# A fused perceiver layer: the Gelu of a small network moved from the scalar engine's table to a polynomial and a tanh, and unread matrix products put into two places

## The reference

```
qk = einsum('bhqd,bhkd->bhqk', Q, K);  scores = qk / sqrt(dk)
feats  = stack([mean(scores), mean(max(scores)), mean(var(softmax(scores)))])   # 3 numbers a head
hidden = gelu(feats @ w1.T + b1, approximate=False)       # 64 wide, erf form
hidden = gelu(hidden @ w2.T + b2, approximate=False)      # 64 wide
t = exp(clip(hidden @ w3.T + b3, log 0.1, log 10))        # one number a head
out = (softmax(qk / (2 t)) @ V) @ Wo.T + bo
```

## Time and profile before

| what | us |
|---|---|
| median of 3 runs | 1217.95 |
| lowest, highest | 1214.53, 1223.5 |
| profiled execution, first to last instruction (span) | 1213.1 |
| VectorE busy | 812.4 (67%) |
| ScalarE busy | 765.5 (63%) |
| TensorE's mean granted clock | 0.897 |

### The profile page before, as it was taken

The page is one execution under the profiler, slowest core; times in us unless marked ns, Lnnn a source line. Parts: engine busy times, 40 slices in busy tenths (PEclk is TensorE's granted clock), DMA queues, the critical chain, the costliest instruction groups (busy, mean ns, idle before and its releaser), DMA issues.

```text
span 1213.1 us, 39205 instructions
## 1 busy us (share of the span) xinstructions
PE 1101.5 (91%) x14964; PEld 892.8 (74%) x14964; DVE 812.4 (67%) x2128; ACT 765.5 (63%) x1547; POOL 406.0 (33%) x420
## 2 busy tenths in 40 slices
PE   3867799999999999999999999999999999999864
PEld 3535587878888787878878797878787887867743
DVE  4467667566776776677777776577667777578245
ACT  2434576776766676767766776667767676766521
POOL 2268352223232331433232332333143233331223
PEclk9968798987979897989999898989889898989787
DMA  4610010201010111102010111102020100000000
GB/s 132 193 29 27 23 37 4 61 11 42 19 44 21 36 29 28 37 2 54 11 45 20 37 29 29 36 4 61 2 54 11 45 20 19 3 2 6 8 2 9
DMA packets 46812, 38.85 MB, mean 32 GB/s; under 512 B 14576, under 2 KB 46000, under 8 KB 46640
## 3 DMA queue, kind: packets, MB, share of 16 engines
q1 hardware_dynamic: 46640, 36.41, 11.1%
HBM read 34.30 MB, written 2.10 MB: 30 GB/s over the span
## 4 chain that ended last, share of the span: by engine, by line
PE 75%; DVE 12%; issue 5%; ACT 4%; DMA 2%; POOL 1%; SPq 1%; DVEq 0%; ACTq 0%; POOLq 0%
PE pjp L665 14%; PE s1p L704 14%; PE s2p L735 13%; PE pjp L658 12%; PE pvp L752 8%; DVE est L1392 3%; DVE negm L1386 2%; PE tlp L848 2%; PE tlp L866 1%; PE tlp L787 1%; ACT ering L1045 1%; PE tlp L842 1%; PE s2p L725 1%; PE s2p L645 1%; PE tlp L809 1%
## 5 line engine op out<-in xcount | busy, mean ns | idle before, releaser
L1386 DVE TENSOR_REDUCE negm<-s1p 128x1 f32<-128x400 f32 (+1 forms) x512 | 289.8, 566 | 199.1 <-PE s1p L704 196.6
L1045 ACT ACTIVATE ering<-s1p,negm 128x400 f32<-128x400 f32 (+1 forms) x512 | 303.8, 597 | 118.6 <-DVE negm L1386 112.2
L1056 ACT ACTIVATE pring<-s2p 128x512 f32<-128x512 f32 x427 | 240.8, 565 | 148.1 <-PE s2p L735 145.1
L704 PE MATMUL s1p<-kt,qbd 32*128 32x400 f32 (+1 forms) x1024 | 305.2, 608 | 28.1 <-ACT ering L1045 26.1
L1392 DVE BATCH_NORM_STATS2 est<-ering 128x6 f32<-128x400 f32 (+1 forms) x512 | 290.7, 568 | 19.6 <-ACT ering L1045 19.6
L735 PE MATMUL s2p<-q2bd,kt 32*128 32x128 f32 (+1 forms) x3192 | 244.6, 285 | 0.0
L735 PEld LDWEIGHTS s2p<-q2bd,kt 32*128 32x128 f32 (+1 forms) x3192 | 233.3, 194 | 5.8
L658 PE MATMUL pjp<-cr,wkv 128*128 128x256 f32 (+1 forms) x1344 | 192.4, 295 | 29.7 <-DVE vt L1358 19.2
L1264 POOL TENSOR_TENSOR cr<-stage,cr 128x512 fp32r<-128x512 f32 (+1 forms) x112 | 132.1, 1180 | 234.3 <-ACT cr L1036 234.3
L658 PEld LDWEIGHTS pjp<-cr,wkv 128*128 128x128 f32 x1344 | 171.8, 198 | 45.5 <-issue 29.1
L665 PE MATMUL pjp<-wkv,cr 128*128 128x256 f32 (+1 forms) x1200 | 195.7, 318 | 10.0 <-ACT kt L1018 9.8
(11 more groups left out here) (278 smaller groups left out, 1033.1 us busy)
## 6 DMA issues: line engine op xcount, KB each, us to landing
stage<-in_ctx SPq DMA_DIRECT2D x96, 256.0 KB, 3.0
qbd<-q_dram SPq DMA_DIRECT2D x128, 8.0 KB, 1.8
stage<-in_ctx SPq DMA_DIRECT2D x16, 65.0 KB, 2.5
vt<-in_x SPq DMA_DIRECT2D x1, 1024.0 KB, 6.8
q_dram<-late SPq DMA_DIRECT2D x1, 1024.0 KB, 4.6
late<-in_x SPq DMA_DIRECT2D x7, 128.0 KB, 2.3
out_y<-late SPq DMA_DIRECT2D x7, 128.0 KB, 1.8
late<-in_gate SPq DMA_DIRECT2D x1, 768.0 KB, 4.9
```

Source lines behind the costliest of these rows:

```text
L704: nc.tensor.matmul(s1p[u % 3][:, 0:w], qbd[s.par][rows, g, :], kt[s.par][rows, g, lo:lo + w], start=True, stop=True).then_inc(s1_full, 1)
L1045: nc.scalar.activation(ering[:, u % 3, 0:w], s1p[u % 3][:, 0:w], ACT.Exp, bias=negm[s.par][:, p, c:c + 1]).then_inc(s1_exp, 1)
L1056: nc.scalar.activation(ring_place(s, v)[0:m, 0:n], s2_bank(s, v)[0:m, 0:n], ACT.Exp).then_inc(s2_exp, 1)
L1386: nc.vector.tensor_reduce(negm[s.par][:, p, ch:ch + 1], s1p[u % 3][:, 0:w], AX.X, ALU.max, negate=True).then_inc(s1_max, 1)
```

## The change

Gelu is no longer a function of the scalar engine. With v = product + bias, VectorE makes x = v/2, q = 2x² and, by a polynomial of degree 6 in q, y = x·r(q); ScalarE takes tanh(y), and VectorE ends with (tanh + 1)·x. These are 9 operations on VectorE (`GE_N`), 1 on ScalarE and 1 more on VectorE for each of the two layers, on 128x16 tiles. q, the last step of the polynomial and the tanh lie in columns 16 to 47 of bank `tlp`. `w1m`, `w2s`, `w3b` and `hid` are 128 wide in place of 64, with zeros that GpSimd writes in the set-up.

The second layer moves from step 6 to 7, the third from 7 to 9, parts 2 and 3 of the statistics from 8 and 10 to 9 and 11, the exponential between them from 9 to 10. The rounding's operations at position 68 move to 69, step 5 of an odd slot. `keep_clock` issues products of `wkv` with itself into an `s2p` bank that the next `scores2` overwrites: 12 in odd slots and 5 in even ones ahead of the second layer, and 4 at step 13 behind the shift's.

```diff
-STATS_AT = [1, 3, 8, 10]
-MLP_AT = {5: 0, 6: 1, 7: 2}
+STATS_AT = [1, 3, 9, 11]
+MLP_AT = {5: 0, 7: 1, 9: 2}
+FILL_FOR = 8
+FILL_1 = {1: 12, 2: 5}
+FILL_MORE = 4
-W_AT, GELU_AT, C_AT = 2, 5, 9
+W_AT, C_AT = 2, 10
+GELU_AT = [5, 7]
+HALF_R = [2.0 * 2.0 ** k * c for k, c in enumerate(ERF_R)]
+GE_N = len(HALF_R) + 2
+Q_LAST = 69
...
-        w1m = sb("w1m", [P, 3, DH])
+        w1m = sb("w1m", [P, 3, P])
...
+            def keep_clock(s, n, at):
+                s_, v = s.second(at, 0)
+                if s_.has(1, B) and not s_.drains():
+                    need(pe, s2_exp, s_.lin(S2U, v - 1 - S2U))
+                    for _ in range(n):
+                        nc.tensor.matmul(s2_bank(s_, v)[:, 0:D], wkv[:, 0, 0, 0, 0:P], wkv[:, 1, 0, 0, :], start=True,
+                                         stop=True)
...
-                        if step in MLP_AT and s.has(1, B):
-                            temperature(s, MLP_AT[step])
...
-                    if step % 2 == 1 and step in MLP_AT and s.has(1, B):
+                    if step in MLP_AT and s.has(1, B):
+                        if MLP_AT[step] == 1:
+                            keep_clock(s, FILL_1[s.r], FILL_FOR)
                         temperature(s, MLP_AT[step])
+                    if step + 1 == S2_AT[0]:
+                        keep_clock(s, FILL_MORE, step + 1)
...
-            def gelu(s, n):
-                need(act, mlp_full, s.lin(N_MLP, n + 1 - N_MLP))
-                nc.scalar.activation(hid[:, n, :], tlp[0:DH, 0:H], ACT.Gelu,
-                                     bias=col("b1" if n == 0 else "b2", 0, DH)).then_inc(mlp_free, 1)
+            def gelu_tanh(s, n):
+                need(act, ge, s.lin(2 * GE_N, GE_N * (n + 1) - 2 * GE_N))
+                nc.scalar.activation(tlp[:, H:2 * H], gy[:, :], ACT.Tanh).then_inc(ge_th, 1)
...
+            def gelu(s, n, part):
+                x, b = gx[:, n, :], col("b1" if n == 0 else "b2")
+                q, low = tlp[:, H:2 * H], tlp[:, 2 * H:3 * H]
+                if part == 0:
+                    need(dve, mlp_full, s.lin(N_MLP, n + 1 - N_MLP))
+                    c = Chain(ge, s.lin(2 * GE_N, GE_N * n - 2 * GE_N))
+                    c(nc.vector.tensor_scalar(x, tlp[:, 0:H], b, 0.5, ALU.add, ALU.mult))
+                    c(nc.vector.scalar_tensor_tensor(out=q, in0=tlp[:, 0:H], scalar=b, in1=x, op0=ALU.add, op1=ALU.mult))
+                    c(nc.vector.tensor_scalar(gu[:, :], q, HALF_R[-1], HALF_R[-2], ALU.mult, ALU.add))
+                    c(nc.vector.tensor_tensor(gu[:, :], gu[:, :], q, ALU.mult))
+                    for r in HALF_R[-3:0:-1]:
+                        c(nc.vector.scalar_tensor_tensor(out=low if r == HALF_R[1] else gu[:, :], in0=gu[:, :], scalar=r,
+                                                         in1=q, op0=ALU.add, op1=ALU.mult))
+                    c(nc.vector.scalar_tensor_tensor(out=gy[:, :], in0=low, scalar=HALF_R[0], in1=x, op0=ALU.add,
+                                                     op1=ALU.mult), False)
+                    assert c.n == GE_N
+                else:
+                    need(dve, ge_th, s.lin(2, n + 1 - 2))
+                    nc.vector.scalar_tensor_tensor(out=hid[:, n, :], in0=q, scalar=1.0, in1=x, op0=ALU.add,
+                                                   op1=ALU.mult).then_inc(mlp_free, 1)
```

50 lines of the change are left out of this document (32 added, 18 removed).

## The result

The changed kernel takes 1279.74 us, the median of 4 runs (1278.48 to 1283.41), beside 1216.51 us for the kernel before on the same chip (4 runs, 1214.53 to 1223.5). The ratio is 1.0503, with a 95% interval from 1.0464 to 1.0542: 5% slower, where I had forecast 1.6% faster. The profiled execution has a span of 1276.6 us against 1213.1, 63.5 us more.

A forecast was written before the change was run, and what follows sets the result against it. TensorE was taken as the bound (75% of the chain), slowed by low clock around the Gelu waits. 1213.1 - 17.5 (even slots) - 4 (odd) + 2 (batch 16) = 1193.6 us span, plus 4.85: 1198.4 us, range 1192 to 1206.

The forecast's parts named there:

- The replay: Step-by-step timing of batches 8 and 9 after the change; in batch 8 it put unit 11 1.5 us ahead.
- surcharge for PSUM: VectorE's PSUM reads: the skill's 0.065 us an operation, estimated 16 us in all, was left out of the count.
- From there the old kernel spent 1.8 us up to 608.3: Even slots behind unit 11: full clock saves 0.9 and 1.7 us, less 0.55 us for four products; 2.5 us taken.
- the sum: Whole span: seven even slots x 2.5, eight odd x 0.5, batch 16 2 us later; 1193.6 us span, 1198.4 us median.
- Statistics and shift are not late in this: Even slot: part 3 of the statistics ends near 610, some 0.5 us ahead of the shift's turn on TensorE.
- Stand in a wait that is longer, below, and are free: TensorE: the 12 or 5 products ahead of the second layer (1.66 or 0.69 us) cost nothing.
- one more odd slot: Batch 15 was counted among the eight odd slots, each 0.5 us shorter.
- 4.85 us between span and median: Difference added to the forecast span of 1193.6 us to give the forecast median of 1198.4 us.
- The clock still falls behind the second layer: Rival: TensorE's gaps there still lower the clock and products only cost; 10.4 us slower, 1228 us; chance 0.09.
- VectorE as the bound: Rival: 2.25 us a chain and 0.1 us more a hand-over lose 14 us of the gain; 1213 us; chance 0.12.
- Theory A: Follow-up theory, not forecast: the change only moves the half-clock stretch to steps 10 to 13, where it costs much.
- Theory C: Follow-up theory, not forecast: VectorE's chain costs by its own length.

The follow-up runs named there:

- kernel 1: Changed kernel without any of the unread clock-holding products: 1264.84 us, ratio 1.0408.
- 5: Changed kernel without the four unread products at step 13: 1265.59 us, ratio 1.0348.
- 11: 6 (Gelu polynomial of four coefficients, clip's exponential behind) without any unread product: 1202.05 us, ratio 0.987.
- 14: 6 without the four products at step 13, keeping those ahead of the second layer: 1214.44 us, ratio 0.9934.
- kernel 13: kernel 2 (full chain of nine, clip's exponential behind) without any unread product: 1228.67 us, ratio 1.0039.
- 8: kernel 2 without the four products at step 13: 1243.36 us, ratio 1.019.
- kernel 9: Kernel before the change, with only the clip's exponential placed behind the second pass's on ScalarE: 1217.66 us, ratio 0.999.
- Kernel 18: kernel 12 with the clip's exponential back ahead of the second pass's (1254.02 us), plus the third layer ahead of step 9's projection on TensorE: 1234.07 us, ratio 1.0115.
- kernel 2: Changed kernel with the clip's exponential moved behind the second pass's and the first pass's on ScalarE: 1251.15 us, ratio 1.0264.
- 6: kernel 2 with four of seven polynomial coefficients, three VectorE operations fewer per chain, rougher Gelu: 1228.78 us, ratio 1.0049.
- kernel 12: 11 with four coefficients fitted anew, Gelu error below 3e-5, same instructions: 1205.22 us, ratio 0.9826.
- kernel 4: Kernel before the change, old Gelu, with only the unread products added (12 or 5, and 4 at step 13): 1236.59 us, ratio 1.0143.
- kernel 16: kernel 12 with two polynomial coefficients, chains of four operations in place of six: 1215.03 us, ratio 0.9954.
- kernel 3: Changed kernel with nine more unread products in step 10: 1275.18 us, ratio 1.0503.
- kernel 7: kernel 2 with the four unread products moved from step 13 into step 10, ahead of the second pass: 1266.39 us, ratio 1.0368.

## Why the prediction was wrong

**What held.** The chain of nine takes 1.95 us, from 608.87 to 610.82 in batch 8 (1.9 counted); the table loads are gone but for the first; the projection at step 9 takes 1.63 and 1.68 us (1.7 forecast); unit 10 comes 7.5 us behind the first layer in batch 8 (7.7 counted) and unit 11 8.3 us (8.4 counted). The replay was right as far as it went. Unit 11 of the kernel before is at 607.29, where the replay put 606.95, so at that unit the change was 1.9 us ahead, not 1.5. In the changed kernel all ten of a layer's operations read PSUM, where the prediction counted eight. No surcharge for PSUM came out: operations with a column take 0.23 and 0.24 us, the others 0.17, as those with SBUF inputs do. (The Trainium skill, "VectorE: DVE Perf Modes", TRN2 errata, would have them 0.065 us longer from PSUM, the estimate in the prediction; at 16 columns the rows don't show it.)

```profile
608.87 0.23 DVE L1501 TENSOR_SCALAR gx<-tlp,cols 128x16 f32<-128x16 f32 x1 [1.48 <-PE tlp L713]
609.13 0.24 DVE L1502 SCALAR_TENSOR_TENSOR tlp<-tlp,cols,gx 128x16 f32<-128x16 f32 x1
609.41 0.17 DVE L1503 TENSOR_SCALAR gu<-tlp 128x16 f32<-128x16 f32 x1
...
610.65 0.17 DVE L1508 SCALAR_TENSOR_TENSOR gy<-tlp,gx 128x16 f32<-128x16 f32 x1
```

**The step that failed** is the one behind unit 11: "From there the old kernel spent 1.8 us up to 608.3 and 3.4 us from 611.8 at half clock; at full clock these are 0.9 and 1.7 us shorter". I stopped the replay there and took the rest from the kernel before, at a better clock. In its place stands a stretch of 10 us at half clock from 10 us on, and unit 14 comes 20.8 us behind the first layer in batch 8, where the sum had 14.7. From unit 11 to unit 14 it is 12.5 us, where the kernel before took 7.0 and the sum had 6.3. I had read the low clock as a thing of the gap at the second layer. The runs show that filling that gap takes the low clock out of the first 9 us and not out of the batch: kernels 1 and 5, without and with those products, are 1264.8 and 1265.6 us, with 17.1 and 13.7 us at half clock a batch; 11 and 14 have 7.4 and 7.8, 13 and 8 have 8.7 and 11.5. The sum had every even batch 2.5 us and every odd one 0.5 us shorter; batches 4 to 14 are 4.1 us longer in the mean.

**What I left out** is ScalarE's queue in step 10. "Statistics and shift are not late in this" looked only at when part 3 ends, and not at what is queued behind the clip's exponential while it waits; nor at the third layer, which the change puts behind the projection. The wait of that exponential was 25.9 us in the rows before and cost nothing (kernel 9). After the change it is 16.2 us in all and its place costs 28.6 us:

```profile
L1151 ACT ACTIVATE lt<-lt 128x16 f32<-128x16 f32 x16 | 3.5, 216 | 16.2 <-DVE lt L1473 16.2
```

Kernel 18 bears on why: where the wait is over before the projection is, it costs nothing or little; where it comes behind the projection, TensorE wants what is queued. It gives back 20 of the 49 us that the place costs with the short chain.

**The products.** "Stand in a wait that is longer, below, and are free": with the clip's exponential behind, those ahead of the second layer cost 15 us (8 against 13), those of step 13 8 to 14 us (2 against 8, changed against 5, 6 against 14), near the 1.66 or 0.69 and the 0.55 us a batch of their own time (26 us over 15 batches). So they give back about nothing, but for one pair: with the clip's exponential ahead the second layer's products come out even (1 against 5).

**The sum, redone** by medians, in one order of undoing: clip's exponential 28.6 us (changed to 2), step 13's products 7.8 (2 to 8), the second layer's 14.7 (8 to 13), and what is left against the kernel before 8.8 us (1228.67 to 1219.89); with 3.4 us between the two measurements of the kernel before these make the 63.2. The steps lie between groups, and that of 7.8 is within the runs' spread. In another order the parts are others: without products the exponential's place is worth 36 us (1 against 13), and with it in the wrong place the second layer's products are worth 0.8 (1 against 5). The slot of batch 15, which I had counted as one more odd slot, is 11.2 us longer, and from batch 16's first layer to the end it is 9.0 us more, where I had 2. There the clip's exponential comes 8.2 us behind the first layer in place of 4.7, and the low clock is 19.7 us longer. These 20 us are part of those sums and were not taken apart. Of the 4.85 us between span and median about 3 are luck of the profiled execution: every later one has its own time 1.8 to 2.2 us above its span.

**The rivals.** "The clock still falls behind the second layer" named a fall of the clock that makes it slower, but in the wrong place, and priced it at 10 us. "VectorE as the bound" priced 0.1 us a hand-over and 14 us in all; the chain from nine to six operations alone is worth 23 us (13 against 12), 5 us more than its own 18, which is within the runs' spread. Theory A holds for the place of the low clock, but for kernel 4, and for a part of the time. Theory C holds for most of the chain. Neither held alone, and neither had the queue.

**What stays open.** Why kernel 16 with two operations less is at half clock for 17 us in five of the batches 4 to 14, and kernel 12 in one. I have no run that tells what lets the clock fall there. Nor is it shown whether the late fall in the changed kernel comes from the hole in step 10 alone: kernel 3 filled it, and in batches 9 to 13 the clock fell all the same; in kernel 2 TensorE's wait there is gone, and it fell too. Nor why batch 15 alone takes 58.5 to 60.6 us in seven of the kernels and 63 to 74 in the others.

## What to carry to other kernels

When a step is moved, follow it through every engine's queue until the old and the new order are in step again, and ask of each wait whether it is still over before another engine wants what is queued behind it. A wait of 26 us in the rows can be free, and after a move of one step a shorter one can cost 2%. Products that only hold the clock earned more than their time in no pair of kernels here; it was better to leave the low clock where the engine waits anyway. The Gelu by way of tanh was worth doing, with no products, six operations in place of nine and the clip's exponential behind the queue: 1205.2 us against 1219.9, a ratio of 0.9826 (0.9746 to 0.9906).

## What the runs showed of the hardware that I had not expected

A stretch at half clock costs by what lies in it. In batch 9 of the changed kernel the work between 693.3 and 703.6 lost an estimated 4.6 us, by comparing its rows with their like at full clock (2.77 for 1.53, 1.11 for 0.65, 1.70 for 0.94, 1.54 for 0.93, and so on); batch 9 of kernel 1 lost 1.4 us to unit 10 by 6.8 us of it (10.3 against 8.9 us).

The time is no smooth function of a wait. Some kernels spread over 19 to 26 us from run to run (kernel 7: 1249.86 to 1275.61, kernel 13: 1211.84 to 1230.55), while the changed kernel and kernels 2 and 5 stay within 5 us in four runs each. In the changed kernel six of the batches 4 to 14 have the same 10.2 us at half clock behind 9 us, in kernel 13 they differ from 0 to 12.0 us; that this makes the spread is not shown.
